# A packed graph kernel: rows of four blocks alternate, degree counted while packing, 256-column products in layer 1, verdict before the last product, one block of engine programs

## The reference, cut to what matters

```
adj0 = adj * (y @ y.T)                               # y: one-hot class of each node
s    = (adj0 / max(sum(|adj0|, axis=1), 1e-12)) @ x
x    = layernorm(x + 0.9 * s + 0.1 * h0)
filt = tanh(adj * adj) * (adj > 0)                   # keep the 350 largest of a row
h2   = tanh(x @ W_proj + b_proj)
x    = layernorm(x + relu(topk_350(filt) @ (h2 @ W_gcn) + b_gcn))
```

## Time and profile before

| what | value |
|---|---|
| median of 3 runs | 478.86 us |
| profiled execution | 478.8 us, of which the span of instructions is 477.0 us |
| TensorE (PE) busy | 449.3 us, 94% |
| VectorE (DVE) busy | 378.9 us, 79% |
| ScalarE (ACT) busy | 262.7 us, 55% |
| GpSimd (POOL) busy | 159.5 us, 33% |
| DMA | 108.50 MB, busy in the first 22 of 40 slices |
| mean granted clock of TensorE | 0.985 |

### The profile page before, as it was taken

How to read it: one execution, slowest core, us unless ns; L and a number is a source line. 1 busy time by engine, 2 the same in 40 slices (tenths; PEclk the granted TensorE clock), 3 DMA queues, 4 the chain that set the end, 5 groups by cost and what they waited for, 6 DMA issues and landing times.

```text
span 477.0 us, 15332 instructions
## 1 busy us (share of the span) xinstructions
PE 449.3 (94%) x5104; PEld 391.1 (82%) x5104; DVE 378.9 (79%) x1401; ACT 262.7 (55%) x353; POOL 159.5 (33%) x309
## 2 busy tenths in 40 slices
PE   3669999999999999999999999999999999999990
PEld 2448888989998899889998878888888888888880
DVE  5889999999999999999999866566566566566552
ACT  4988999999999999999999826300000000000000
POOL 3012544445555554444555431221221221221220
PEclk9988999999999999999999999999999999999996
DMA  8999999999999999999998000000000000000000
GB/s 267 406 419 418 402 419 393 384 416 417 414 416 416 421 418 422 420 419 421 419 415 326 8 0 1 19 11 17 17 11 17 17 11 17 17 11 17 17 18 10
DMA packets 28254, 108.50 MB, mean 227 GB/s; under 512 B 5401, under 2 KB 18226, under 8 KB 18226
## 3 DMA queue, kind: packets, MB, share of 16 engines
q1 hardware_dynamic: 28226, 108.14, 56.6%
HBM read 105.57 MB, written 2.56 MB: 227 GB/s over the span
## 4 chain that ended last, share of the span: by engine, by line
PE 88%; DVE 5%; DMA 2%; issue 2%; ACT 1%; POOL 1%; POOLq 0%; DVEq 0%; SPq 0%; ACTq 0%
PE acc L492 73%; PE words L443 8%; PE proj_acc L571 3%; PE feat_acc L555 2%; DMA a_rows<-in_adj_dram 2%; DVE a_bits L746 2%; PE xnt_acc L547 1%; DVE g_words L302 1%; POOL pack_half L373 1%; DVE turned L830 1%; ACT count_out L648 1%; DVE x_parts L775 0%; PE gram_acc L475 0%; DVE y_diag L760 0%; DVE same_class L850 0%
## 5 line engine op out<-in xcount | busy, mean ns | idle before, releaser
L492 PE MATMUL acc<-x_parts,turned 128*128 128x257 f16 (+1 forms) x1600 | 195.8, 277 | 0.7 <-DVE x_parts L775 0.7
L648 ACT ACTIVATE count_out<-a_rows,ones 128x2688 bf16<-128x2688 f32 (+1 forms) x80 | 190.0, 2375 | 0.5
L492 PEld LDWEIGHTS acc<-x_parts,turned 128*128 128x128 fp8e4 (+1 forms) x1600 | 157.0, 99 | 25.9 <-DVE x_parts L775 1.2
L492 PE MATMUL acc<-f_parts,turned 128*128 128x257 f16 (+1 forms) x1560 | 175.4, 273 | 0.0
L492 PEld LDWEIGHTS acc<-f_parts,turned 128*128 128x128 fp8e4 (+1 forms) x1560 | 151.2, 97 | 23.2 <-issue 0.4
L746 DVE TENSOR_SCALAR a_bits<-a_rows 128x2688 bf16<-128x2688 f32 (+1 forms) x80 | 116.7, 1459 | 3.3 <-DMA a_rows<-in_adj_dram 2.9
L830 DVE TENSOR_SCALAR turned<-a_words 128x320 uint16 (+1 forms) x305 | 66.9, 233 | 58.7 <-PE acc L492 58.4
L400 POOL TENSOR_TENSOR var_eps<-mean_var,consts 128x1 f32<-128x1 f32 x80 | 18.5, 231 | 272.6 <-DVE mean_var L1036 143.2
L403 POOL TENSOR_TENSOR rstd<-var_eps,consts 128x1 f32<-128x1 f32 x80 | 86.0, 1075 | 6.3
L830 DVE TENSOR_SCALAR turned<-same_class 128x320 uint16<-128x320 uint16 x313 | 71.2, 253 | 0.1
L443 PEld LDWEIGHTS words<-pack,a_bits 128*128 128x128 bf16 (+1 forms) x1600 | 53.6, 96 | 10.3 <-DVE a_bits L746 6.7
(11 more groups left out here) (109 smaller groups left out, 289.9 us busy)
## 6 DMA issues: line engine op xcount, KB each, us to landing
a_rows<-in_adj_dram SPq DMA_DIRECT2D x39, 1344.0 KB, 8.1
a_rows<-in_adj_dram SPq DMA_DIRECT2D x39, 1156.0 KB, 8.6
h_rows<-in_L_gnn_h_dram SPq DMA_DIRECT2D x39, 64.0 KB, 6.1
out_dram<-xn SPq DMA_DIRECT2D x39, 64.0 KB, 1.5
xs<-in_x_dram SPq DMA_DIRECT2D x3, 640.0 KB, 10.0
xs<-in_x_dram SPq DMA_DIRECT2D x1, 512.0 KB, 9.0
y_nat<-in_L_gnn_y_dram SPq DMA_DIRECT2D x1, 304.0 KB, 3.6
a_rows<-in_adj_dram SPq DMA_DIRECT2D x1, 84.0 KB
```

The costliest lines, as they stand in the source:

```text
L492: mm = pe.matmul(acc[par][0:m, 0:PARTS], bits, parts[:, b, 0:PARTS], start=first and b == blocks[0], stop=last and b == blocks[-1])
L648: act.activation(count_out[0:m, 0:w], a_rows[par][h][0:m, 0:w], ACT.Relu, bias=ones[0:m, 0:1], scale=-HUGE, accum_out=col).then_inc(s_coun ...
```

## The change

- Rows alternate between four blocks: blocks 0 to 2 share 384 rows (TRIO), then each four blocks 512 rows; the last is as before. y, x and h0 are loaded with pieces of four rows (256 B, 2 KB, 2 KB; three rows in the first). h0 comes once in four blocks. The stationary operand of packing steps by 4 elements. The pieces of `adj` are now 2432 and 2568 columns (HB is 19 instead of 21).
- SP and GpSimd run layer 0 in loop bodies of 8 steps (`steps8`).
- `pack` gets a ninth column of ones: each packing matmul also gives the number of ones. Words lie at a pitch of 10 (PITCH), 8 words, the count, and one unused.
- `f_parts` has 256 columns a block, with no constant; the products of layer 1 have 256 columns. The degree copies (L1011) are gone. ScalarE sums the counts of all blocks in one activation, and VectorE compares this sum with what the counted zeros demand.
- The checks stand in steps 3 and 4 of layer 1, the matmul of the verdict ahead of the last block's product, the flag in step NB.
- Both paths are in one block of engine programs: each engine waits for the flag (`s_flag`) and loads it when its own packed work is issued. SP waits for the stores of the output last.

```
-    HB = NB // 2 + 1
+    HB = NB // 2 - 1
+    TRIO = 3
+    PITCH = WORDS + 2
...
-        v = a[P:FULL * P, cols].rearrange("(s p e) c -> e s p c", p=P, e=2)[(par + 1) % 2]
+        v = a[TRIO * P:FULL * P, cols].rearrange("(s p e) c -> e s p c", p=P, e=4)[place(c)]
...
-        f_parts = sb("f_parts", [P, NB, PARTS + 1], F16)
+        f_parts = sb("f_parts", [P, NB, 2 * F], F16)
...
-                    mm = pe.matmul(words[par][0:k, b * WORDS:(b + 1) * WORDS],
+                    mm = pe.matmul(words[par][0:k, b * PITCH:b * PITCH + WORDS + 1],
                                    a_bits[h][0:m, c:c + (k - 1) * d + 1:d], pack[0:m, :], start=True, stop=True)
...
+                cols = PARTS if parts is x_parts else 2 * F
...
+                if isinstance(t, int) and t == LAST:
+                    pe.wait_ge(s_good, CHECKS)
+                    pe.matmul(feat_acc[0:1, 0:1], verdict[:, :], ones[:, 0:1], start=True, stop=True)\
+                        .then_inc(s_sum, 1)
                 for h in range(2):
                     multiply(t + NB, par, rows_of(t), f_parts, h)
             steps(pe, step1, 0)
-            pe.wait_ge(s_good, CHECKS)
-            pe.matmul(feat_acc[0:1, 0:1], good[:, :], ones[:, 0:1], start=True, stop=True)\
-                .then_inc(s_sum, 1)
...
+            act.wait_ge(s_words, NB)
+            act.wait_ge(s_measured, 4)
+            act.activation(count_out[:, 0:NB * NB].rearrange("p (n b) -> p n b", b=NB),
+                           a_words[:, :, :].rearrange("p n (b w) -> p n b w", w=PITCH)[:, :, :, WORDS],
+                           ACT.Copy, accum_out=ones_in[:, :]).then_inc(s_measured, 1)
...
+                if isinstance(t, int) and t == 3:
+                    check_counts()
+                if isinstance(t, int) and t == 4:
                     check_sums()
+                if isinstance(t, int) and t == NB:
+                    dve.wait_ge(s_sum, 1)
+                    dve.tensor_scalar(flag[:, :], feat_acc[0:1, 0:1], 0.0, 0.0, ALU.is_equal, ALU.is_equal)\
+                        .then_inc(s_flag, 1)
...
         @block.sync
         def _(sp):
+            sp.wait_ge(s_flag, 1)
             bad = sp.value_load(flag[0:1, 0:1], min_val=0, max_val=1)
...
+            sp.wait_ge(s_stored[0], 16 * (NB // 2))
+            sp.wait_ge(s_stored[1], 16 * (NB // 2))
```

More of the change, by code:

```diff
@@ L34, with packed_path @@
 PART_MAX = 32768.0
-def packed_path(nc, x, adj, h0, y, w_proj, b_proj, w_gcn, b_gcn, out, flag):
+def packed_path(nc, engines, sem, x, adj, h0, y, w_proj, b_proj, w_gcn, b_gcn, out, flag, s_flag, s_out):
     N, F = x.shape
@@ L180, in packed_path @@
         zeros_in = sb("zeros_in", [P, 2 * NB])
-        degree = sb("degree", [P, NB])
+        ones_in = sb("ones_in", [P, 1])
+        need_in = sb("need_in", [P, 1])
+        surplus = sb("surplus", [P, 1])
+        verdict = sb("verdict", [P, 1])
         x_sums = sb("x_sums", [P, NB])
@@ L333, in _ @@
             for q, part in enumerate(X_PART):
-                lo, hi = max(part.start, 1), min(part.stop, FULL)
-                sp.dma_start(pair_view(xs, lo, hi), pairs_of(x, lo, hi)).then_inc(s_in[f"x{q}"], 16)
+                lo, hi = max(part.start, TRIO), min(part.stop, FULL)
+                sp.dma_start(quad_view(xs, lo, hi), quads_of(x, lo, hi)).then_inc(s_in[f"x{q}"], 16)
             sp.dma_start(xs[0:TAIL, FULL, :], x[FULL * P:N, :]).then_inc(s_in["xt"], 16)
-            load_rows(1, 1, 0)
+            load_rows(1, 1, 0, 1)
@@ L343, in _, with step, store @@
             sp.dma_start(bg_row[:, :], b_gcn.rearrange("(a p) -> a p", a=1)).then_inc(s_in["bg"], 16)
-            def step(t, par, pair):
+            def step(t, par, pair, i, c):
                 if not isinstance(t, int) or t >= 2:
[L347 to L352, removed]
+                    load_rows(t, par, i, c)
+                if valid(t - 1) and c > TRIO and place(c - 1) == 0:
+                    load_h0(t - 1, i, c - 1)
+            steps8(sp, step, 4, TRIO + 8)
+            def store(t, par, pair, i, c):
                 m = rows_of(t)
                 sp.wait_ge(s_result, t + 1)
[L355 to L358, removed]
+                sp.dma_start(rows_in(out, t, i, c, slice(0, F)), xn[par][0:m, :]).then_inc(s_out[par], 16)
+            steps8(sp, store, 0, TRIO)
         @engines.gpsimd
@@ L420, in _ @@
             pool.wait_ge(s_in["xt"], 16)
-            steps(pool, step, LAG)
+            steps8(pool, step, LAG, LAG)
             def step1(t, par, pair):
@@ L1462, in gnn_kernel, with sem @@
 def gnn_kernel(nc, x, adj, h0, y, w_proj, b_proj, w_gcn, b_gcn, out):
-    with nc.sbuf_tensor("flag", [1, 1], I32) as flag:
-        packed_path(nc, x, adj, h0, y, w_proj, b_proj, w_gcn, b_gcn, out, flag)
-        general_path(nc, x, adj, h0, y, w_proj, b_proj, w_gcn, b_gcn, out, flag)
+    with nc.sbuf_tensor("flag", [1, 1], I32) as flag, ExitStack() as sems, nc.Block() as engines:
+        def sem(name):
+            return sems.enter_context(nc.semaphore(name))
+        s_flag = sem("s_flag")
+        s_out = [sem(f"s_out{p}") for p in range(2)]
+        packed_path(nc, engines, sem, x, adj, h0, y, w_proj, b_proj, w_gcn, b_gcn, out, flag, s_flag, s_out)
+        general_path(nc, engines, sem, x, adj, h0, y, w_proj, b_proj, w_gcn, b_gcn, out, flag, s_flag, s_out)
 _INS = ['x', 'adj', 'L0_gnn_h0', 'L0_gnn_y', 'L1_gnn_W_proj', 'L1_gnn_b_proj', 'L1_gnn_W_gcn', 'L1_gnn_b_gcn']
```

206 lines of the change are left out of this document (123 added, 83 removed).

## The result

The changed kernel takes 483.34 us (median of 6 runs, 482.17 to 484.25) against 478.75 us of the kernel before on the same chip. The ratio is 1.0092, with a 95% interval of 1.0070 to 1.0115. 468.7 was forecast, with 466.0 to 473.7 as the range: the prediction was wrong, and on the wrong side.

A forecast was written before the change was run, and what follows sets the result against it. PE was taken to bound both layers, with about 2% to spare on VectorE in layer 0. Terms -5.1 (256 columns), -5.2 (early verdict) and +0.2 (verdict's matmul) summed to -10.1: 468.7 us, range 466.0 to 473.7.

The forecast's parts named there:

- Packing with 9 columns: 0: Packing matmuls: a ninth column and a stationary read stepping 8 B instead of 4 cost nothing, pace staying 25 ns.
- the packing gets slower: Rival, layer 0 packing: the 8 B step halves the read's rate, 25 ns more a matmul, +39 us, 508; chance 0.06.
- 256 columns, -5.1: Layer 1 products: 256 columns instead of 257 save 3.2 ns on each of 1600, 5.1 us.
- the cause named then: Layer 1 products: `f_parts` rows of 514 B start every 516 B, afterwards both are 512 B; 3.2 ns a product taken.
- One block, early verdict, -5.2: Kernel end: flag written in step NB, PE's fetch beside the last store; span ends at 471.8 instead of 477.0.
- a fetch stays at the end: Rival, kernel end: SP or VectorE jumps late over its general code; 3.9 us come back at most, 472.6; chance 0.12.
- Checks and ScalarE's sum, 0: Layer 1, steps 3 and 4: checks and ScalarE's sum, below 2 us, cost nothing, hidden by VectorE's waits and double-buffered products.
- without cover: Layer 1 check: should one product, 4.5 us, not cover VectorE's wait for ScalarE's sum, it would cost about 1.
- words at a pitch of 10: ScalarE's copy and VectorE's mask and unpacking: no change, 0; slower strided words were a rival, 489, chance 0.04.
- the pieces of 2432 and 2568: Casts of `adj` in pieces of 2432 and 2568 columns: 0, since the sum of columns is the same.
- larger DMA pieces (0): h0 and x transfers: fewer, larger pieces gain 0, since PE sets layer 0's pace and loads don't bound the start.
- slower loads: Rival, layer 0 loads: rows four apart slow them; from 4% the gain is gone, 476 to 480; chance 0.04.

The follow-up runs named there:

- experiments 1 and 3: 1: measuring-only kernel timing packing matmuls and products; 3: changed kernel with rows in pairs, 472.33 us, then that with only packing reads at 8 B steps, 483.25 us.
- experiment 1: Measuring-only kernel, none of the reference's work: packing matmuls at several steps and column counts, products at several row pitches; 33.2 ns at step 4, 25.0 at step 2.
- the first probe: Measuring-only kernel with bf16 stationary operand of 128 elements at steps of 1 to 16, and products at several row pitches; 59.9 ns at step 8.
- the second probe: Measuring-only kernel with stationary operand in fp8 at steps of 1 to 16 B, or bf16 of only 64 elements; fp8 at 8 B 33 ns.

## Why the prediction was wrong

**The step that failed** is "Packing with 9 columns: 0". It said that a stationary read with a step of 8 B "could stay, or the read could take twice as long and be seen in full, 25 ns more; I take 0, since 8 columns and their weights have room in 25 ns". There was no such room. The 25 ns are a floor that steps of 2 and 4 B reach, a step of 6 B already takes 26.2, and at 8 B the read sets the pace with 33.2. The cost was 8.2 ns for each matmul at that step, 12 us in all, shown by experiments 1 and 3; the kernel without it (472.33) lies 3.6 us over the forecast.

The rival "the packing gets slower" was the right one, and it got 6 in 100. It had the mechanism and not the size: 25 ns more a matmul and 508 us, where 8.2 ns and 483 were measured. Its own threshold stood in the text: from 32 ns on the loss outweighs the gain. The reason against it ("25 ns are far from what 8 columns need") took the gap between work and pace for slack, though nothing in the profile said what filled it. An unexplained 25 ns where columns need 3 is a sign that something else is the limit, and the change touched just the operand that was left.

I had set a rule beside it, of the Trainium skill (SBUF — State Buffer, Specifications): a 16-byte line needs two hits or more for full bandwidth. I read it as two being enough, and so a step of 8 B passed. The runs disagree with that for this read: two hits a line take 33.2 ns against 25.0 with four, and from there on each line more costs the same, whether lines have two hits or, at 16 B, one. What they bear out is the line of 16 bytes, and the other half of the same entry, that each cross to a new line pays a penalty: from 64 lines on that is 0.42 ns a line.

**256 columns, -5.1:** the mechanism was right, the size less so. 2.6 ns a product by the two traces (111.9 less 109.3), 4.2 us over 1600. The 3.2 came from bf16 same-class matmuls at 108.3 ns in a row of six; the product at 256 columns takes 109.1 to 109.3. The rule of the Trainium skill (TensorE: Matmul & The Clock Gate, Back-to-back issue gap) gives 109.2 for 256 columns, and here the trace agrees; for 257 it gives 109.6, which is 0.4 short of aligned rows (110.0) and 2 ns short of rows every 516 B. So the cause named then, the rows' start, carries 1.1 to 1.7 of the 2.5 ns of experiment 1, and the 257th column the rest.

**One block, early verdict, -5.2:** -4.1. PE's jump went under cover as forecast. VectorE's came last instead: it loads the flag only behind its last xn. The arrivals at the final meeting show it (count, ns, us from the start), TensorE's in the kernel before, then TensorE's and VectorE's in the changed one:

```profile
L1077 PEldq DRAIN  x1: 71/71/71, 476.7 to 476.7; - x1
```
```profile
L1526 PEldq DRAIN  x1: 73/73/73, 475.8 to 475.8; - x1
L1526 DVEq DRAIN  x1: 58/58/58, 480.0 to 480.0; - x1
```

The others were there by 473.3 before, and by 478.6 now. VectorE's branch over its general code stands at 477.2, so 2.8 us pass until it arrives. The rival "a fetch stays at the end" came true by a part, 1.1 us of its 3.9.

**Checks and ScalarE's sum, 0:** +1.0, the price named for "without cover". ScalarE's sum was taken to be below 2 us, by its rate on float32 without a stride. It took 3.11 us, 1.94 ns an element. It reads one uint16 in ten; in the same trace a sum of 2560 float16 in a row takes 2.34 us, 0.91 ns an element, so the stride is the likely cause, though no run varies it alone. The cover of one product, 4.5 us, was there, but the sums before it ran to 312.4 and the check waited in step 4 until 315.7.

Put on the forecast, the four add up: 468.7 + 12 + 0.9 + 1.1 + 1.0 = 483.7 us, against 483.34 measured.

**Right as taken:** words at a pitch of 10 (unpacking still 232 ns), the pieces of 2432 and 2568, larger DMA pieces (0), no slower loads.

## What to carry over

Where an instruction is slower than its count of columns says, find what fills the time before you call it slack; the first change to the other operand may find it for you. A layout that makes transfers neater also sets the step at which engines read, and that is paid at every read: here four rows a piece bought nothing and cost 12 us. And once two engines are within a few per cent, a gain on one is kept only down to the other.

## What the hardware showed unexpectedly

- The pace of a stationary read goes by the 16-byte lines that it touches: with 128 elements 25.0 ns up to 32 lines, 26.2 at 48, 33.2 at 64, 39.9 at 80, 46.5 at 96, 59.9 at 128 (61.4 when the step is 32 B, 61.9 for fp8 at 16 B). From 64 to 128 lines each line is 0.42 ns.
- This pace does not follow TensorE's granted clock. 128 elements at 16 B (L144 of the first probe) take 60.0 ns at a granted clock of 1.00 (126 to 130 us) as at 0.50 (131 to 133 us). In the group at L146 of the second probe it stayed at 120 ns while the granted clock fell from 1.00 (2.4 GHz) to 0.50 (1.2 GHz):

```profile
134.10:138.00 3.90, 3.90 (x34) 1.00 0.02 4
138.00:142.00 4.00, 4.00 (x36) 0.54 0.00 0
142.00:148.50 6.50, 6.50 (x56) 0.50 0.00 0
```

- A stationary operand of 64 columns is slower than one of 128: 31.8 ns against 25.0 when dense, 60 against 33 at 8 B, 120 against 60 at 16 B. In the kernel, the matmul with 8 columns started 96 ns after the one before it, and 25 with a pad of zeros.
- Moving rows of 257 float16 that start every 516 B take 1.7 ns a product more than rows every 528 B.
